# The attention pass of a macaron layer on one core: orders of all engines, PSUM banks and loop borders set anew

## The reference

```python
x = x + 0.5 * ffn(_layernorm(x))        # top 8 of 64 slots, slots summed over all rows, GRU, slots read back
x = x + attn(_layernorm(x))
x = x + 0.5 * ffn(_layernorm(x))
# attn, 16 heads of 32; q and k are l2-normalized, a and b are sigmoids of x @ Wa + ba and x @ Wb + bb
def step(state, inp):
    q_t, k_t, v_t, a_t, b_t = inp
    pred = jnp.einsum('bhde,bhd->bhe', state, k_t)
    error = v_t - pred
    update = jnp.einsum('bhe,bhd->bhde', b_t[..., None] * error, k_t)
    state = a_t[..., None, None] * state + update
    return (state, jnp.einsum('bhde,bhd->bhe', state, q_t))
y = _rmsnorm(y, g_norm) * _silu(x @ Wg)  # over the 512 columns
return y @ Wo
```

## Time and profile before

| | |
|---|---|
| median of 3 runs | 2670.61 us (2669.8 to 2679.14) |
| the profiled execution: its own time, its span | 2676.29 us, 2674.5 us |
| PE, VectorE, ScalarE, GpSimd busy | 94%, 68%, 39%, 51% of the span |
| attention pass from the first to the last `cum` (31 steps) | 354.1 to 2490.4 us: 68.91 us for a step |
| mean granted clock of TensorE over the span | 0.975 |

### The profile page before, as it was taken

How to read it: one execution, slowest core, us unless ns; L and a number is a source line. 1 busy time by engine, 2 the same in 40 slices (tenths; PEclk the granted TensorE clock), 3 DMA queues, 4 the chain that set the end, 5 groups by cost and what they waited for, 6 DMA issues and landing times.

```text
span 2674.5 us, 117064 instructions
## 1 busy us (share of the span) xinstructions
PE 2524.0 (94%) x51035; PEld 1788.1 (67%) x51035; DVE 1821.2 (68%) x5308; ACT 1050.8 (39%) x1962; POOL 1357.9 (51%) x1895
## 2 busy tenths in 40 slices
PE   7999879999999999999999999999999999999768
PEld 6788546666666666666666666666666666666544
DVE  7778456777666776667676667777677767677626
ACT  5777323333333333333333333333333333333220
POOL 2222155555556655555566665555555555555410
PEclk9999989999999999999999999999999999999869
DMA  7334022222222222222222222222222222222278
GB/s 232 109 109 149 16 62 71 71 69 69 67 67 69 68 70 66 72 72 72 72 72 72 69 70 61 62 69 72 68 69 72 72 72 72 72 72 71 64 262 329
DMA packets 440719, 233.70 MB, mean 87 GB/s; under 512 B 352336, under 2 KB 368784, under 8 KB 440208
## 3 DMA queue, kind: packets, MB, share of 16 engines
q1 hardware_dynamic: 430992, 209.44, 28.7%
q10 hardware_dynamic: 9216, 16.78, 1.7%
HBM read 125.49 MB, written 74.97 MB: 75 GB/s over the span
## 4 chain that ended last, share of the span: by engine, by line
PE 78%; DVE 8%; issue 5%; POOL 4%; ACT 2%; SPq 1%; DMA 1%; POOLq 0%; DVEq 0%; ACTq 0%
PE psum L881 26%; PE psum L936 8%; PE psum L1060 8%; PE psum L1078 5%; PE psum L1041 4%; PE psum L1021 3%; PE psum L988 3%; PE psum L1028 3%; PE psum L727 3%; PE psum L790 2%; PE psum L972 1%; PE psum L953 1%; PE psum L872 1%; POOL dm L2107 1%; PE psum L1098 1%
## 5 line engine op out<-in xcount | busy, mean ns | idle before, releaser
L881 PE MATMUL psum<-w_all,xnT 128*128 128x512 f32 (+2 forms) x2048 | 740.1, 502 | 1.9 <-ACT xnT L1687 1.4
L2036 POOL TENSOR_TENSOR sm<-sm,half 128x1 f32<-128x1 f32 (+1 forms) x384 | 536.4, 1397 | 70.3 <-ACT sm L1731 54.2
L881 PEld LDWEIGHTS psum<-w_all,xnT 128*128 128x128 f32 x2048 | 366.5, 191 | 219.3 <-issue 169.1
L2610 DVE TENSOR_TENSOR blk<-blk 128x30 f32<-128x30 f32 (+14 forms) x960 | 327.5, 341 | 73.7 <-issue 47.1
L2612 DVE TENSOR_TENSOR blk<-blk 128x30 f32<-128x30 f32 (+14 forms) x960 | 323.8, 337 | 33.0
L2068 POOL TENSOR_SCALAR sm<-sm 128x1 f32<-128x1 f32 x64 | 22.5, 351 | 557.6 <-DVE sm L2516 557.6
L936 PEld LDWEIGHTS psum<-xnT,w_all 128*128 128x128 f32 x2048 | 245.0, 194 | 58.1 <-issue 49.2
L936 PE MATMUL psum<-xnT,w_all 128*128 128x128 f32 x2048 | 275.4, 285 | 0.8 <-issue 0.6
L1060 PE MATMUL psum<-w_out,gate 128*128 128x512 f32 x512 | 259.5, 621 | 0.1
L1041 PE MATMUL psum<-qg,st 32*32 32x64 f32 x8192 | 175.1, 220 | 25.9 <-DVE st L2629 13.2
L1041 PEld LDWEIGHTS psum<-qg,st 32*32 32x32 f32 x8192 | 133.6, 106 | 68.2 <-DVE st L2629 39.3
(11 more groups left out here) (287 smaller groups left out, 4594.1 us busy)
## 6 DMA issues: line engine op xcount, KB each, us to landing
blk<-n_scratch SPq DMA_DIRECT2D x64, 512.0 KB, 4.0
xin<-in_L_attn_x_dram SPq DMA_DIRECT2D x96, 256.0 KB, 2.8
n_scratch<-nn SPq DMA_DIRECT2D x64, 256.0 KB, 4.3
xh<-xc SPq DMA_DIRECT2D x64, 256.0 KB, 2.6
e_scratch<-blk SPq DMA_DIRECT2D x32, 512.0 KB, 2.8
x_scratch<-xh SPq DMA_DIRECT2D x62, 256.0 KB, 2.6
rxn<-in_L_attn_x_dram SPq DMA_DIRECT2D x32, 256.0 KB, 3.2
pk<-kdt SPq DMA_DIRECT2D x128, 64.0 KB, 2.2
```

Source lines behind the costliest of these rows:

```text
L881: last = mm(dst, xnT[b][:, k * P:(k + 1) * P], w_all[:, k * WK + at:k * WK + at + n], start=(k == 0), stop=(k == KC - 1))
L2036: return g.tensor_tensor(dst, a, half[:, 0:n], ALU.pow)
L2610: own(tt(o, Y[:, 0:rows, s_:s_ + 1].to_broadcast([P, rows, cols]), N[:, s_:s_ + 1, s_ + 1:CH].to_broadcast([P, rows, cols]), ALU.mult))
```

## The change

The same calls are made on every engine, each as often as before; only `fill(55, 1)` becomes `fill(45, 1)`. What differs:

- the table of PSUM banks, and with it the `free` waits and some others (`gram` of batch 1 waits for `draw` of batch 0 only, or for other readers, as its new banks 3 and 0 want; `dec` of batch 1 has no wait of its own);
- the order inside `step_sp`, `step_pe`, `step_act`, `step_pool`, `step_dve`, and the place where one step ends and the next begins (`step_*(o, p, q, r, s)` for `t` from 4, with `first_*` and `last_*` changed to match);
- on SP, `load_alpha` and `load_first` run a pair further ahead (`o`), and `key_across` and `beta_across` earlier.

A line that leaves the step at one end and isn't entered anew is at the other end of the loop body (`hidden(s, 1, 1)`, for instance). The core of the diff, with the indentation cut:

```diff
-xT_at = [banks(0, 1), banks(6, 1)]
-k_at = [banks(0, 1), banks(3, 1)]
-q_at = [banks(2, 1), banks(1, 1)]
-va_at = [banks(7, 1), banks(1, 1)]
-vb_at = [banks(5, 1), banks(2, 1)]
-g_at = [banks(2, 1), banks(5, 1)]
+xT_at = [banks(0, 1), banks(1, 1)]
+k_at = [banks(7, 1), banks(0, 1)]
+q_at = [banks(5, 1), banks(5, 1)]
+va_at = [banks(2, 1), banks(4, 1)]
+vb_at = [banks(0, 1), banks(0, 1)]
+g_at = [banks(5, 1), banks(2, 1)]
 dec_at = [banks(0, 1), banks(4, 1)]
-ones_at = [banks(5, 1)[:, 0:1], banks(6, 1)[:, 0:1]]
-wo_at = [banks(2, 1), banks(7, 1)]
-rxT_at = [banks(3, 1), banks(6, 1)]
-h_at = [banks(1, 1), banks(3, 1)]
-lg_at = [banks(1, 1)[:, 0:NS], banks(1, 1)[:, 0:NS]]
-y_at = [banks(5, 2), banks(6, 2)]
-cum_at = banks(6, 1)[:, 0:8 * H]
-aT_at = banks(6, 1)[:, 0:P]
-slot_at = banks(2, 1)
-gram_at = [[banks(2, 1), banks(7, 1)], [banks(0, 1), banks(4, 1)]]
-uw_at = [[banks(6, 1), banks(4, 1)], [banks(3, 1), banks(7, 1)]]
-gq_at = [[banks(4, 1), banks(0, 1)], [banks(3, 1), banks(1, 1)]]
+ones_at = [banks(6, 1)[:, 0:1], banks(6, 1)[:, 0:1]]
+wo_at = [banks(2, 1), banks(5, 1)]
+rxT_at = [banks(4, 1), banks(6, 1)]
+h_at = [banks(1, 1), banks(6, 1)]
+lg_at = [banks(1, 1)[:, 0:NS], banks(4, 1)[:, 0:NS]]
+y_at = [banks(6, 2), banks(6, 2)]
+cum_at = banks(7, 1)[:, 0:8 * H]
+aT_at = banks(0, 1)[:, 0:P]
+slot_at = banks(5, 1)
+gram_at = [[banks(2, 1), banks(1, 1)], [banks(3, 1), banks(0, 1)]]
+uw_at = [[banks(6, 1), banks(1, 1)], [banks(5, 1), banks(7, 1)]]
+gq_at = [[banks(3, 1), banks(1, 1)], [banks(1, 1), banks(4, 1)]]
...
-def step_sp(p, q, r, s, u):
-    inverse_in(r, 1)
-    key_across(r, 1)
-    store_alpha(u)
-    load_alpha(p)
-    beta_across(q)
-    coupling_out(q, 0)
-    coupling_out(q, 1)
+def step_sp(o, p, q, r, s):
     coupling_in(q)
+    key_across(q, 0)
     store_second(r, 0)
-    load_first(p, 0)
-    key_across(q, 0)
     hold(q, 0)
+    store_alpha(s)
     store_second(r, 1)
-    load_first(p, 1)
+    key_across(q, 1)
     hold(q, 1)
+    load_alpha(o)
+    load_first(o, 0)
     inverse_out(q)
+    load_first(o, 1)
     inverse_in(q, 0)
+    beta_across(p)
+    inverse_in(q, 1)
...
             pe.wait_ge(S["xnT"], both(n, b))
         if b == 1:
-            free((n, (S["gate"], both(n, 0))))
+            free((n, (T["pt"][1], nth(n, 1))))
     last = project(b, W_V + D // 2, D // 2, vb_at[b][:, 0:D // 2], (2 * part, 2 * part + 1))
     if part == 1:
         last.then_inc(S["vb_ps"], 1)
     if part == 0:
...
-            free((n - 1, (S["yv"], both(n - 1, 0))), (n, (S["vb"], both(n, 0))))
+            free((n - 1, (S["x2"], both(n - 1, 0))), (n, (T["pt"][0], nth(n, 0))))
     for k in range(KC):
         at = k * WK + W_G + part * P
         last = mm(g_at[b][:, part * P:(part + 1) * P], w_all[:, at:at + P], xnT[b][:, k * P:(k + 1) * P],
         last.then_inc(S["g_ps"], 1)
...
         mm(cum_at[:, 2 * k * H:2 * (k + 1) * H], mask[:, :], gla[:, :], start=(k == 0), stop=False, skip_group_check=True)
     for hq in range(NC):
     last.then_inc(S["cum_ps"], 1)
 def dec(n, b):
-    pe.wait_ge(S["rhsd"], both(n, b))
+    if b == 0:
+        pe.wait_ge(S["rhsd"], both(n, b))
+    if b == 0:
+        free((n, (S["kn"], both(n, 1))))
     for part, mask in enumerate((after, cross)):
         last = mm(dec_at[b][:, part * D // 2:(part + 1) * D // 2], mask[:, :], dr[b][:, part * D // 2:(part + 1) * D // 2],
                   start=True, stop=True)
 def gram(n, b, piece):
     if piece == 0:
-        pe.wait_ge(S["kt"], both(n, b))
...
     for k in range(2 * piece, 2 * piece + 2):
         for part in range(2):
             h = part * H // 2 + k
     if piece == 0:
         pe.wait_ge(e_in[b], 48 * n)
         if b == 0:
-            free((n, (T["pt"][1], nth(n, 1))))
+            free((n - 1, (S["hT"], both(n - 1 + NT, 1))))
+        if b == 0:
+            free((n + 1, (S["xnT"], both(n + 1, 1))), (n - 1, (S["top"], both(n - 1 + NT, 0))), (n, (T["pt"][0], nth(n, 1))))
         else:
-            free((n + 1, (T["pt"][0], nth(n + 1, 1))), (n - 1, (S["x2"], both(n - 1, 1))))
+            free((n + 1, (S["e4"], n + 1)), (n, (S["ysq"], both(n, 0))))
     for k in range(2 * piece, 2 * piece + 2):
         for part in range(2):
             h = part * H // 2 + k
                 last.then_inc(T["uw_ps"][b], 1)
 def qe_T(n, b, part):
-    if b == 1:
-        pe.wait_ge(S["qe"], both(n, b))
     if part == 0:
+        if b == 0:
+            free((n + 1, (S["x1"], both(n + 1, 1))), (n, (T["pt"][1], nth(n, 0))))
+        else:
+            free((n + 1, (T["pt"][0], nth(n + 1, 1))), (n, (T["qg"][0], nth(n, 1))))
+    else:
...
-    fill(55, 1)
+    fill(45, 1)
     first_xT(1, 0)
...
-def step_pe(p, q, r, s, u):
+def step_pe(o, p, q, r, s):
+    hidden(s, 1, 1)
+    proj_vb(q, 0, 0)
+    qe_T(r, 0, 0)
+    first_xT(q, 1)
+    proj_vb(q, 0, 1)
+    proj_va(q, 1, 0)
     proj_va(q, 1, 1)
     apply_uw(r, 0, 0)
     apply_uw(r, 0, 1)
     apply_uw(r, 0, 3)
     proj_k(q, 1, 0)
     proj_k(q, 1, 1)
-    qe_T(r, 0, 0)
     qe_T(r, 0, 1)
     apply_gy(r, 0, 0)
     apply_gy(r, 0, 1)
     proj_k(q, 1, 2)
     proj_q(q, 1, 0)
     proj_k(q, 1, 3)
+    apply_gy(r, 0, 3)
     proj_q(q, 1, 1)
-    apply_gy(r, 0, 3)
     proj_q(q, 1, 2)
     proj_q(q, 1, 3)
     gram(q, 0, 0)
+    gram(q, 0, 1)
+    gram(q, 0, 2)
+    gram(q, 0, 3)
     chain(r, 0, 0)
-    gram(q, 0, 1)
     chain(r, 0, 1)
-    gram(q, 0, 2)
+    dec(q, 0)
     chain(r, 0, 2)
-    dec(q, 0)
+    dec(q, 1)
     chain(r, 0, 3)
-    gram(q, 0, 3)
-    dec(q, 1)
     gram(q, 1, 0)
     gram(q, 1, 1)
     gram(q, 1, 2)
     gram(q, 1, 3)
+    out_proj(r, 0, 0)
     logits(s, 1)
+    y_norm(r, 0)
     cum(q)
-    out_proj(r, 0, 0)
     out_proj(r, 0, 1)
+    qe_T(r, 1, 0)
     apply_uw(r, 1, 0)
     apply_uw(r, 1, 1)
     apply_uw(r, 1, 2)
     apply_uw(r, 1, 3)
     out_proj(r, 0, 2)
-    qe_T(r, 1, 0)
+    out_proj(r, 0, 3)
     qe_T(r, 1, 1)
-    y_norm(r, 0)
-    out_proj(r, 0, 3)
     apply_gy(r, 1, 0)
-    apply_gy(r, 1, 1)
     slots(s)
     proj_g(q, 1, 0)
     proj_g(q, 0, 0)
+    apply_gy(r, 1, 1)
     apply_gy(r, 1, 2)
     apply_gy(r, 1, 3)
     proj_g(q, 0, 1)
     proj_g(q, 1, 1)
     proj_g(q, 1, 2)
     chain(r, 1, 0)
-    last_xT(r, 0)
+    ffn(p)
     chain(r, 1, 1)
     proj_g(q, 0, 2)
-    ffn(p)
     proj_g(q, 0, 3)
     chain(r, 1, 2)
+    proj_vb(q, 1, 0)
+    last_xT(r, 0)
+    chain(r, 1, 3)
+    proj_vb(q, 1, 1)
     proj_g(q, 1, 3)
-    chain(r, 1, 3)
     hidden(r, 0, 0)
-    proj_vb(q, 1, 0)
+    hidden(r, 0, 1)
+    out_proj(r, 1, 0)
     first_xT(p, 0)
-    hidden(r, 0, 1)
-    proj_k(p, 0, 0)
-    out_proj(r, 1, 0)
     out_proj(r, 1, 1)
+    out_proj(r, 1, 2)
     y_norm(r, 1)
-    out_proj(r, 1, 2)
     out_proj(r, 1, 3)
     alpha_T(s)
+    proj_k(p, 0, 0)
     proj_k(p, 0, 1)
-    proj_vb(q, 1, 1)
     proj_va(p, 0, 0)
     proj_k(p, 0, 2)
+    proj_q(p, 0, 0)
+    proj_q(p, 0, 1)
+    logits(r, 0)
+    proj_k(p, 0, 3)
+    proj_q(p, 0, 2)
+    proj_q(p, 0, 3)
+    last_xT(r, 1)
     proj_va(p, 0, 1)
-    proj_q(p, 0, 0)
-    proj_k(p, 0, 3)
-    logits(r, 0)
-    last_xT(r, 1)
-    proj_q(p, 0, 1)
-    proj_q(p, 0, 2)
     hidden(r, 1, 0)
-    proj_q(p, 0, 3)
-    proj_vb(p, 0, 0)
-    hidden(r, 1, 1)
-    first_xT(p, 1)
-    proj_vb(p, 0, 1)
-    proj_va(p, 1, 0)
 first_pe()
-for t in range(5, NT + 1):
-    step_pe(t, t - 1, t - 2, t - 3, t - 4)
+for t in range(4, NT):
+    step_pe(t + 1, t, t - 1, t - 2, t - 3)
...
+def step_act(o, p, q, r, s):
+    move_vb(q, 0)
+    gates_exp(q)
+    move_uw(r, 0, 0)
+    move_uw(r, 0, 1)
     gates_ln(q)
     move_va(q, 0)
-    move_va(q, 1)
     key_square(q, 1)
     move_gq(r, 0, 0)
     move_gq(r, 0, 1)
+    move_va(q, 1)
     query_square(q, 1)
     dec_exp(q, 0)
     dec_exp(q, 1)
+    y_square(r, 0)
     last_exp(s, 0)
-    y_square(r, 0)
+    y_mean(r, 0)
...
+def step_pool(o, p, q, r, s):
+    decay_rows(q, 0)
+    decay_rows(q, 1)
+    beta_mask(q, 1)
+    beta_mask(q, 0)
     key_power(q, 1)
     query_power(q, 1)
-    beta_mask(q, 1)
     decay_mask(q, 0)
     decay_mask(q, 1)
     y_pairs(r, 0)
     chunk_decay(r, 1)
+    y_power(r, 0)
+    query_decayed(q, 0)
+    key_decayed(q, 0)
+    alpha_sums(s)
+    key_decayed(q, 1)
     chunk_decay(q, 0)
     key_written(q, 0)
-    key_decayed(q, 0)
-    y_power(r, 0)
-    query_decayed(q, 0)
-    key_decayed(q, 1)
+    query_decayed(q, 1)
     last_rstd(r, 0)
     first_rstd(p, 0)
     y_pairs(r, 1)
     y_power(r, 1)
+    key_written(q, 1)
     last_rstd(r, 1)
     first_rstd(p, 1)
...
+def step_dve(o, p, q, r, s):
     gates_decay(q)
     query_scale(q, 0)
     key_sums(q, 1)
-    key_turn(q, 0)
     chunk_kept(r, 0, 0)
+    chunk_kept(r, 0, 1)
     query_turn(q, 0)
-    chunk_kept(r, 0, 1)
     query_sums(q, 1)
+    key_scale(q, 1)
     state(r, 0, 0)
+    key_turn(q, 1)
     state(r, 0, 1)
     state(r, 0, 2)
-    key_scale(q, 1)
-    key_turn(q, 1)
     query_scale(q, 1)
     query_turn(q, 1)
     state(r, 0, 3)
     last_moments(r, 0)
```

(14 more changed lines are left out.)

849 lines of the change are left out of this document (416 added, 433 removed).

## The result

The changed kernel takes 2709.87 us (median of 4, 2706.94 to 2716.24), the one before 2670.2 in the same comparison. The ratio is 1.0149, 95% interval 1.0115 to 1.0184: slower, by 39.7 us where +20 was forecast, inside the range, but above the forecast's own 2684 to 2705. The profiled execution took 2711.01 us, its span is 2709.2.

What follows compares the result with a forecast made beforehand. PE was taken as the bound, so only its waits, chiefly for instruction packets, could change; 0.2 + 0.35 + 0.15 = +0.7 us a step over 29 steps, +20 us, gave a median of 2691, range 2650 to 2714.

Steps and rivals of the forecast that it cites:

- the forecast's own 2684 to 2705: Whole kernel: range of the main case, packets at the price of 3.6 us, 2691 us; chance 0.35.
- The bound and the ledger: Whole step: PE bounds, 67.1 of 68.91 us; with its calls unchanged, only its waits, idle 1.8 us, can move the time.
- gram(q, 1): Batch 1 gram: draw's 0.77 us wait goes, start 0.56 earlier, packet idle 1.0 at gram(q, 1, 3), end 0.5 later.
- apply_uw(r, 1): Call after gram(q, 1) and the projections: 0.2 us later by equal work, bounds 0.3 earlier to 0.6 later.
- y_norm: y_norm(r, 0) ahead of cum: costs nothing if the gram packet is late, otherwise about 0.6 us, up to 1.2.
- apply_uw(r, 0): Packets behind this one-block call: the next 0.2 us late, then the one after again; +0.35 us a step (0 to 0.9).
- Later borders: Borders from apply_uw(r, 1, 2) to the end of apply_gy(r, 1, 0), during the inverse's transfers: +0.15 us a step (-0.1 to +0.5).
- Asked for when the sequencer enters a block: All packet borders: the next packet is requested on block entry, one block ahead, usable 3.6 us later, up to 5.2 among transfers.
- What costs nothing: Other engines' orders and earlier loads: values PE reads come 0.4 us or more early; if 1 us later, PE pays 0.6.
- the dear rival: Packets at 4.5 us, gram(q, 1) costing 0.9 more: +1.5 us a step, 2714 us; chance 0.08.
- Faster: Rival: packets asked for earlier, not behind chain 3's waits; -0.65 us a step, 2652 us; chance 0.25.
- fill: fill 55 to 45, ahead of the loop: PE waits for the first pair anyway; shifted borders already counted in the places named.

Runs made afterwards that it cites:

- after_halfin: Changed kernel with coupling_in moving only half the rows (2 x 256 KB for 2 x 512 KB) from the second pair on, input partly stale: 2704.97 us, ratio 1.0141.
- after_g0: Changed kernel with proj_g(q, 0, 0) and apply_gy(r, 1, 1) swapped on PE: 2707.82 us, ratio 1.0131 to the kernel before.
- after_g0_58: Changed kernel with proj_g(q, 0, 0) and apply_gy(r, 1, 1) swapped, fill(58, 1), and reading(q, 1, 1) ahead of first_sum(p, 0): 2671.36 us, ratio 0.9987.
- before_logits: Kernel before with logits(s, 1) moved between dec(q, 1) and gram(q, 1, 0): 2671.97 us, ratio 1.0016.
- after_fill77: Changed kernel with fill(77, 1) in place of fill(45, 1), all borders 128 instructions earlier: 2896.46 us, ratio 1.0876 to the kernel before.
- before_fill45: Kernel before with fill(45, 1) in place of fill(55, 1), its borders 40 instructions later: 2848.36 us, ratio 1.0702.
- before_halfin: Kernel before with coupling_in moving only half the rows from the second pair on, the rest of the inverse's input stale: 2652.19 us, ratio 0.9923.
- before_copy: Kernel before with coupling_in loading the inverse's input once and VectorE copying it to yblk, computation whole: 2658.71 us, ratio 0.9967.

## Why the prediction was right, and where it wasn't

- **The bound and the ledger: right.** PE's work stayed (67.1 to 66.9 us a step), its idle time made the whole difference.
- **`gram(q, 1)`: right in place, too high in its idle, and wrong in one premise.** The wait for `draw` went, `gram(q, 1)` starts 6.87 us after `gram(q, 0)` (mean; 6.7 forecast, 7.44 before), and the packet is late 4 instructions into `gram(q, 1, 3)`. The mean idle is 0.43 us (up to 1.3) where 1.0 was said, and another 0.2 is lost in `gram(q, 0, 3)`. The premise was that this packet is asked for only when the states of chain 2 are there, at 32.4, and usable 3.6 later. It starts 0.35 us (median) after they are there, where one that nothing delays starts about 1.0 after it can be asked for: it was asked for before, and in 10 of 25 steps nothing is idle here at all. In the step shown it is used at 1187.62, which is 35.35 on the prediction's clock (1179.57, the start of `gram(q, 0)`, is 27.30) and not 36.0 to 36.2. The 3.45 us of the kernel before were also nearer to the edge than I read: the list in the earlier trace rows has only idles over 0.15 us; with the shorter ones PE idles at that border in 13 of 26 steps, 0.1 us a step. `apply_uw(r, 1)` comes 12.92 behind `gram(q, 0)`, 12.55 before, with 0.4 of moved work in it: 0 by equal work, +0.2 forecast. `y_norm` waits in some steps, 0.15 a step, where I had it as nothing.
- **`apply_uw(r, 0)`: right in its sum.** +0.35 forecast, 0.15 and 0.2 in the two places named; 0.32 and 0.05 measured.
- **"Later borders": the step that failed.** +0.15 (to +0.5) was said, +0.96 measured, in every step. I had read the price of that packet from the earlier trace rows, 5.2 us with transfers about, and kept it for the new border. The transfer was the cause before. In the changed kernel it was a wait that shows in no list, since PE never idled for it: the sequencer's, for the slot copy, 24 instructions behind the new border and 192 behind the old. "Asked for when the sequencer enters a block" was the wrong sentence: a wait 24 instructions behind the border held the request (after_halfin, after_g0), so it comes some way into the block. How far, and which waits hold it, stays open.
- **"What costs nothing": wrong for one bank.** `proj_vb(q, 1)` waits for `reading(q, 1, 1)`, 0.28 us a step. I had looked at the values that PE reads, and not at this entry of the new bank table.
- The terms as measured, 0 + 0.37 + 0.96 + 0.28 = 1.6, stand against +1.39 of the step.
- **Luck.** The step moved by twice what was forecast (+1.39 for +0.7), and the measured time lies in the range only because the range took in the dear rival's 2714. What was missed is the held request (+0.8 a step) and the bank (+0.3); that `gram(q, 1)` cost 0.2 less than said took a little of it back by chance.
- **The rivals.** "Faster" rested on packets asked for early; what the Trainium skill says ("Runtime: NRT & Kernel Launch", section Instruction fetch mechanics), that crossing a block is mostly hidden, holds for 7 of the 12 borders here, and at the other 5 PE idles 2.3 us a step. The dearer case (+1.5, 2714, chance 0.08) came nearest to the number, but not by its own way: it put the cost into `gram(q, 1)`, which was cheaper than forecast.
- **`fill`: the places of the borders had it in them, but it wasn't priced by itself.** With 58 the changed orders are 0.4% slower, with 45 1.5%: most of the loss is this one number.

## What to carry to other kernels

In this unrolled program PE's code arrives in packets of 256 instructions, and the place of their borders is part of the schedule. Where an engine issues many small matmuls, look for the same: count them, look for blocks with under 3.6 us of work and for waits in the first half of a block, and try a few dozen useless instructions ahead of the loop before judging a new order. Read the waits in the source as well as the engine's idle time: a wait that costs no idle can still hold the next packet. And price a wait by what stands behind it, not by its own length: of 1.2, 0.7 and 0.4 us of idle a step taken away here (after_g0, after_g0_58, before_logits), 0.2, 0.3 and 0 reached the end.

## What the runs showed of the hardware

- A packet of 16 KB that nothing holds and nothing covers costs a block of 1.4 us of small matmuls another 2.2 to 2.5 us (after_fill77): about 3.9 us from block to block. The transfer itself is mostly 1.0 to 1.1 us of it. It starts about 1.0 us after the wait that held it (1.03 in the changed kernel, 1.1 to 1.2 in before_fill45), and PE goes on 1.2 to 1.6 us after the transfer's end.
- Two transfers of 512 KB that run at the same time push its start from 1.0 to 2.0 us (median; before against before_halfin, and before_copy, where one of them is gone, has 0.95).
- An idle of 2.57 us in a busy stretch (after_fill77) lies in 5 us with a granted clock of 0.77, and the next 5 have 0.89; one of 1.84 us in the changed kernel is followed by the lower level too (0.66 from 1060 to 1065), its other idles, up to 1.57 us, are not. Nor does each long one bring it: in after_fill77 28 of 62 idles over 1.0 us, some of 2.4 us, were not followed by it. Where it came, the idle cost what it lasted and the slow matmuls behind it: 1.7 us for the six of L884.
